# Transposing four block rows of the gated matrix between the node steps, and running 28 chunks ahead of the products

## The reference, cut to what matters

```python
h = relu(h @ W1 + b1) @ W2 + b2
x = x + relu(h)                       # end of layer 3
h = maximum(layernorm(x), 0)          # h of layer 4
xp = h @ W_node.T + b_node            # the node product
msg = gate[:, None] * xp[col]         # gate: one number per edge
out = segment_sum(msg, row) / maximum(cnt, 1)[:, None]
return x + out
```

## Time and profile before

| | us |
|---|---|
| runs (3) | 1353.11, 1356.61, 1362.15; median 1356.61 |
| the profiled execution | 1352.15, span 1350.5 |
| end of the paths to the first `turn_g` | 1133.8 to 1168.3 of the span |
| gated loop | 1168.3 to 1341.9 |
| tail: back, scale, store | 1341.9 to 1350.5 |

### The profile page before, as it was taken

How to read it: one execution, slowest core, us unless ns; L and a number is a source line. 1 busy time by engine, 2 the same in 40 slices (tenths; PEclk the granted TensorE clock), 3 DMA queues, 4 the chain that set the end, 5 groups by cost and what they waited for, 6 DMA issues and landing times. The chain is left out here.

```text
span 1350.5 us, 36825 instructions
## 1 busy us (share of the span) xinstructions
PE 1072.0 (79%) x15699; PEld 795.3 (59%) x15699; DVE 969.5 (72%) x1451; ACT 608.5 (45%) x2011; POOL 166.3 (12%) x315
## 2 busy tenths in 40 slices
PE   1495038888888887888888888839999898899997
PEld 1331026666666665666666666539999886655454
DVE  8782158999999999999999999656668724233333
ACT  1202036555555555555555555249996212122222
POOL 4130441211121112111211121000000000000000
PEclk9597557989988989898899999759999998699999
DMA  9523311231122113211321131168000070166641
GB/s 234 123 79 37 47 33 76 99 124 75 75 117 106 75 75 136 88 75 75 135 88 75 75 148 77 74 259 355 2 2 2 1 293 2 50 244 236 242 155 24
DMA packets 37038, 144.85 MB, mean 107 GB/s; under 512 B 21084, under 2 KB 21628, under 8 KB 30204
## 3 DMA queue, kind: packets, MB, share of 16 engines
q1 hardware_dynamic: 31692, 133.20, 27.2%
q0 software_dynamic: 2912, 7.92, 2.3%
q10 hardware_dynamic: 2256, 1.23, 0.4%
HBM read 78.63 MB, written 63.71 MB: 105 GB/s over the span
## 5 line engine op out<-in xcount | busy, mean ns | idle before, releaser
L869 ACT ACTIVATE b_c_row<-b_ps 128x300 bf16<-128x300 f32 (+1 forms) x275 | 114.8, 418 | 235.2 <-PE b_ps L1035 231.3
L1238 PE MATMUL layers_ps<-layers_u,layers_c 128*128 128x192 bf16 x2500 | 210.9, 247 | 8.9 <-ACT layers_u L1417 6.4
L1238 PEld LDWEIGHTS layers_ps<-layers_u,layers_c 128*128 128x128 bf16 x2500 | 208.0, 98 | 14.1 <-DVE layers_y L1546 8.0
L1035 PEld LDWEIGHTS b_ps<-b_mv,b_soh 64*128 64x128 bf16 x9600 | 171.3, 98 | 63.2 <-issue 28.6
L1035 PE MATMUL b_ps<-b_mv,b_soh 64*128 64x50 bf16 (+1 forms) x9600 | 198.4, 193 | 11.5 <-DVE b_mv L948 9.3
L1085 PE MATMUL b_ps<-k_ident,b_a_row 128*128 128x128 f32 x625 | 118.9, 314 | 89.8 <-DVE b_scale L968 88.7
L1035 PE MATMUL b_ps<-b_u_b,b_y 128*128 128x64 f32 x1250 | 165.4, 284 | 12.5 <-DVE b_y L982 12.2
L1085 PEld LDWEIGHTS b_ps<-k_ident,b_a_row 128*128 128x128 f32 x625 | 75.0, 155 | 156.5 <-DVE b_scale L968 128.1
L1035 PEld LDWEIGHTS b_ps<-b_u_b,b_y 128*128 128x128 f32 x1250 | 151.5, 196 | 18.8 <-DVE b_y L982 15.2
L948 DVE TENSOR_TENSOR b_mv<-b_mv,b_parts 128x2808 bf16<-128x2808 bf16 x100 | 149.3, 1493 | 0.0
L1693 DVE COPY layers_c<-layers_ps 128x512 f32<-128x512 f32 (+1 forms) x87 | 55.4, 636 | 117.8 <-PE layers_ps L1372 117.8
(11 more groups left out here) (237 smaller groups left out, 1142.4 us busy)
## 6 DMA issues: line engine op xcount, KB each, us to landing
g_blocks<-b_g_row SPq DMA_DIRECT2D x25, 1600.0 KB, 8.8
layers_c<-g_blocks SPq DMA_DIRECT2D x25, 1600.0 KB, 6.9
c_blocks<-b_c_row SPq DMA_DIRECT2D x25, 800.0 KB, 3.4
layers_c<-c_blocks SPq DMA_DIRECT2D x12, 1600.0 KB, 26.4
prep_attr<-in_edge_attr SPq DMA_DIRECT2D x1, 5642.0 KB
rec<-sort_rec SPq DMA_DIRECT2D x1, 1209.0 KB, 9.3
layers_c<-c_blocks SPq DMA_DIRECT2D x1, 800.0 KB, 24.9
k_xs<-in_x SPq DMA_DIRECT2D x1, 768.0 KB
```

Source lines behind the costliest of these rows:

```text
L869: nc.scalar.activation(out, src[:, :, at, :, :], ACT.Copy).then_inc(s["evac"], 1)
L1035: return nc.tensor.matmul(out, lhsT, rhs, start=start, stop=True, skip_group_check=True)
L1238: return nc.tensor.matmul(out_, lhsT, rhs, start=start, stop=True, skip_group_check=True)
```

## The change

`turn_g` and `use` of PE are defined ahead of the last steps of layer 3. Chunks 0 to 27 (block rows 0 to 3) are transposed between those steps and the node product's, into banks 0 to 3; `gt` grows from 4 to 32 places, and `across` moves behind it. The zero products that open banks 0 to 3 come after the last of these copies. PE's node steps are reordered too: the `turn` of group q + 1 stands ahead of `node(q)`. ACT and DVE copy the early chunks between their own steps, and DVE's three count instructions (L1676 to L1678) move behind them. The loop transposes q + 28 and q + 29 before it uses q and q + 1.

```diff
+AHEAD, KEEP = 28, 32
...
-        gt = [flat[:, RING * NP + 512 * i:RING * NP + 512 * i + 512] for i in range(4)]
-        across = flat[:, RING * NP + 2048:RING * NP + 4096].rearrange("p (k n) -> p k n", k=4)
+        gt = [flat[:, RING * NP + 512 * i:RING * NP + 512 * i + 512] for i in range(KEEP)]
+        across = flat[:, RING * NP + 512 * KEEP:RING * NP + 512 * KEEP + 2048].rearrange("p (k n) -> p k n", k=4)
...
@@ PE
-            turn(6, 6, "z")
-            first(5, 5)
-            first(6, 6)
-            output(5)
-            output(6)
-            for q in range(4):
-                turn(7 + q, q, "h")
-                node(q)
-            for q in range(4, 7):
-                turn(7 + q, q, "h")
-                node(q)
-            pe.wait_ge(s["took"], 4 * NP2)
-            for bank in range(4):
-                mm(ps[:, bank, :]...zeros16..., True)
...
+                bank = q % 4 + (0 if q < AHEAD else 4)
                 for j in range(nh):
-                    ins = nc.tensor.transpose(ps[:, 4 + q % 4, P * j:P * j + P], rows[b % RING][:, h0 + j, :], k["ident"][:])
+                    ins = nc.tensor.transpose(ps[:, bank, P * j:P * j + P], rows[b % RING][:, h0 + j, :], k["ident"][:])
...
+            turn(6, 6, "z")
+            pe.wait_ge(s["took"], 4 * NP2)
             turn_g(0)
             turn_g(1)
+            first(5, 5)
+            turn_g(2)
+            first(6, 6)
+            turn(7, 0, "h")
+            turn_g(3)
+            output(5)
+            turn_g(4)
+            output(6)
+            turn_g(5)
+            for q in range(7):
+                if q < 6:
+                    turn(8 + q, q + 1, "h")
+                turn_g(6 + 3 * q)
+                turn_g(7 + 3 * q)
+                node(q)
+                turn_g(8 + 3 * q)
+            turn_g(AHEAD - 1)
+            copied(AHEAD - 2)
+            copied(AHEAD - 1)
+            for bank in range(4):
+                mm(ps[:, bank, :]...zeros16..., True)
+            pe.wait_ge(s["turned"], 14)
+            pe.wait_ge(s["read"], 14)
             for q in range(0, len(steps), 2):
-                for after in (q + 2, q + 3):
+                for after in (q + AHEAD, q + AHEAD + 1):
                     if after < len(steps):
                         turn_g(after)
@@ ACT
+            def keep(q):
+                n, bank = P * CHUNKS[steps[q][1]][1], q % 4 + (0 if q < AHEAD else 4)
+                act.wait_ge(s["turn_g"], q + 1)
+                if q >= KEEP:
+                    act.wait_ge(s["used"], q - KEEP + 1)
+                nc.scalar.activation(gt[q % KEEP][:, 0:n], ps[:, bank, 0:n], ACT.Copy).then_inc(s["act_g"], 1)
+
             take(6, 1)
+            keep(0)
             hide(5)
+            keep(2)
             hide(6)
+            take(7, 4)
+            keep(4)
             square(5)
-            take(7, 4)
+            take(8, 4)
             root(5)
-            for q in range(1, 7):
-                take(7 + q, FOURS[q][1])
+            for q in range(7):
+                if 0 < q < 6:
+                    take(8 + q, FOURS[q + 1][1])
+                for g in (6 + 3 * q, 7 + 3 * q, 8 + 3 * q):
+                    if g % 2 == 0:
+                        keep(g)
+            for q in range(AHEAD, len(steps), 2):
+                keep(q)
@@ DVE (keep as on ACT, with tensor_copy and dve_g)
+            keep(1)
+            keep(3)
+            output(5)
+            output(6)
+            centre(5)
+            keep(5)
+            vary(5)
+            norm(5)
+            for q in range(7):
+                for g in (6 + 3 * q, 7 + 3 * q):
+                    if g % 2:
+                        keep(g)
+                node(q)
+                if (8 + 3 * q) % 2:
+                    keep(8 + 3 * q)
+            keep(AHEAD - 1)
             c(v.tensor_reduce(t[:], counts...))
             c(v.tensor_scalar(t[:], t[:], 1.0, None, ALU.max))
             c(v.reciprocal(dis[:], t[:]))
-            output(5)
-            output(6)
-            centre(5)
-            node(0)
-            vary(5)
-            node(1)
-            norm(5)
-            for q in range(2, 7):
-                node(q)
+            for q in range(AHEAD + 1, len(steps), 2):
+                keep(q)
```

More of the change, by code:

```diff
@@ L1343, in _ @@
             paths(pe, narrow, wide)
-            turn(6, 6, "z")
-            first(5, 5)
-            first(6, 6)
-            output(5)
-            output(6)
-            for q in range(4):
-                turn(7 + q, q, "h")
-                node(q)
-            for q in range(4, 7):
-                turn(7 + q, q, "h")
-                node(q)
-            pe.wait_ge(s["took"], 4 * NP2)
-            for bank in range(4):
-                mm(ps[:, bank, :].rearrange("p (a n) -> p a n", a=4), k["zeros16"][:], k["zeros16"][:, None, :].to_broadcast([P, 4, P]), True)
-            pe.wait_ge(s["turned"], 14)
-            pe.wait_ge(s["read"], 14)
             def copied(q):
@@ L1379, in use @@
                 n, low = P * nh, F * (i % 2)
-                mm(ps[low:low + F, i // 2, 0:n], y[:, b, :], gt[q % 4][:, 0:n], False).then_inc(s["used"], 1)
+                mm(ps[low:low + F, i // 2, 0:n], y[:, b, :], gt[q % KEEP][:, 0:n], False).then_inc(s["used"], 1)
             def back(bank):
@@ L1387, in back @@
                 ins.then_inc(s["turn_g"], 1)
+            turn(6, 6, "z")
+            pe.wait_ge(s["took"], 4 * NP2)
             turn_g(0)
             turn_g(1)
+            first(5, 5)
[18 more added lines that the diff above has]
+            for bank in range(4):
+                mm(ps[:, bank, :].rearrange("p (a n) -> p a n", a=4), k["zeros16"][:], k["zeros16"][:, None, :].to_broadcast([P, 4, P]), True)
+            pe.wait_ge(s["turned"], 14)
+            pe.wait_ge(s["read"], 14)
             for q in range(0, len(steps), 2):
-                for after in (q + 2, q + 3):
+                for after in (q + AHEAD, q + AHEAD + 1):
                     if after < len(steps):
@@ L1675, in _, with keep @@
             paths(dve, narrow, wide)
+            def keep(q):
+                n, bank = P * CHUNKS[steps[q][1]][1], q % 4 + (0 if q < AHEAD else 4)
+                dve.wait_ge(s["turn_g"], q + 1)
+                if q >= KEEP:
+                    dve.wait_ge(s["used"], q - KEEP + 1)
+                v.tensor_copy(gt[q % KEEP][:, 0:n], ps[:, bank, 0:n]).then_inc(s["dve_g"], 1)
+            keep(1)
[14 more added lines that the diff above has]
+            keep(AHEAD - 1)
             c(v.tensor_reduce(t[:], counts[:, :, :].rearrange("p b s -> p s b"), AX.X, ALU.add))
```

## The result

Four runs of the changed kernel have a median of 1337.55 us (1334.74 to 1340.08), four of the kernel before 1355.15 (1353.11 to 1362.15). The ratio is 0.986, with an interval of 0.982 to 0.990: the kernel is faster, by 1.4%. The forecast was 1340 in 1333 to 1356.6.

A forecast was written before the change was run, and what follows sets the result against it. PE alone was taken to pace the gated loop. Savings of 13.1 + 3.7 + 1.5 = 18.3 us, less 3 for half clock, gave 15.3: 1336.9 from the profiled execution, 1341.3 from the median, written 1340, range 1333 to 1356.6.

The forecast's parts named there:

- The 13.1 us of 100 transpositions: Gated loop: 100 transpositions, priced by distance of starts and not by length, leave PE's loop and save 13.1 us.
- The products cost the same in the last two periods, 1 us either way: Loop's last two periods of 14 chunks, without transpositions: products still cost 7.2 us per period, uncertain by 1 us.
- The waits in the seam: Stretch ahead of the gated loop: PE waits 0.4, 0.7, 1.4 and 0.7 us; at full clock the loop starts 3.7 earlier.
- The clock: Seam: one fall near 1148 or already after the branch's gap, a rise before the loop; two half-clock spells, 3 us.
- The sum: Whole kernel: 18.3 us at full clock less 3 for half clock, 15.3 us saved; 11 to 17 us, chance 0.40.
- The signs: First gated product at 1165 to 1170, seam clock 0.6 to 0.95, loop 159 us, longest wait node(1) for DVE's read.
- A (full clock): Rival: full clock throughout the seam, 18.3 us saved; chance 0.30.
- C (transpositions only moved): Rival: half clock throughout the seam, so the transpositions only move, 0 us saved (0 to 6); chance 0.25.
- D (half clock into the loop): Rival: half clock goes on into the loop, slower, each 4 us there costing 2.0 more; chance 0.05.
- Loads and copies cost nothing: Seam and loop: the 28 copies fit idle ACT and DVE time, loads have 15 us to spare; cost nothing.

The follow-up runs named there:

- fillers: The changed kernel with eight products of zeros queued on PE ahead of the branch: 1334.57 us, ratio 0.987 to the kernel before; again on another chip 1331.22, 0.985.
- e1_late: The changed kernel with its 28 early chunks transposed in one run behind the node steps, lead of 28 kept: 1345.88 us, ratio 0.997 to the kernel before.
- e0_after: The first profiled execution of the changed kernel, with no further edit: 1338.97 us.
- e4_batch: The runs of four: the changed kernel's loop transposes four chunks, then uses four, not two and two: 1322.53 us, ratio 0.979 to the kernel before.
- the best one: The changed kernel with zero products ahead of the branch, DVE's last norm moved later, and four chunks per run in the loop: 1321.15 us, ratio 0.976.

## Why the prediction was right

**The 13.1 us of 100 transpositions.** Right. PE's work in the seam was forecast at 26.0 us with them and measured 26.16 at full clock (fillers). In one run, partly at half clock, the 100 took 13.55 in the trace of e1_late; by length, at 0.27 each, they would have been 27. Reading the start and not the length is what carried the sum.

**The products cost the same in the last two periods, 1 us either way.** Wrong in size: 3.3 us less. The step took the 7.2 us per 14 chunks as the price of the products, while part of it is the price of being cut into pairs. The runs of four showed a turn and back as 0.30 us, of which 0.15 lies in the products. The changed loop has about 14 turns fewer, so this explains about 2 of the 3.3 us; the rest is not explained.

**The waits in the seam.** Right in place, cause and nearly in size: forecast 0.7 and 1.4, measured 0.38 and 1.25; the last 0.7, measured 0.58; that for hide(5) 0.4, measured 0.28 at full clock. Full clock was forecast to make the seam 29.2 us; with the fillers it measured 28.67 and 28.6.

**The clock.** The case was right: the prediction named a fall after node(1) or already after the branch's gap, with a rise before the loop, and priced two; both came, each with a rise again. Its size was not. I gave two spells 3 us and they cost 6.0, since each lasted 6.8 us and not the 3.7 of the loop's opening from which the price was taken. That row was read too short: the opening is only the end of a stretch at half clock, and PE had worked without a break since 1166.0, through the last node product and the zero products, 6.0 us and not 3.7. One of the changed kernel's three executions put the two spells together into one. Why the clock falls in one execution and not in another with the same gap (1.29 us at the branch, a fall in e0_after and none in e4_batch) is open.

**The sum.** Two wrong sizes of 3 us each with opposite signs: 15.3 forecast, 16.0 in the profiled execution, 17.6 between the medians. That 1340 lies within 2.5 us of 1337.55 is in part luck: 3.3 us too few for the products and 3.0 too few for the clock cancel.

**The signs.** Of those named ahead, the clock of the seam (0.80) and the longest wait (node(1) for DVE's read) came. The loop was 155.7 us and not 159. The first gated product, at 1173.91, lies outside 1165 to 1170; with the start of the seam 2.8 us later taken off it is 1171.1, about 1 us out, which is the second spell. No sign of wrong reasoning came: the loop lost 17.9 us, and its period of 14 chunks is 13.78 as before (1180.90 to 1194.68).

**The rivals.** A (full clock) is what the fillers make; it is not what the change does. C (transpositions only moved) and D (half clock into the loop) did not come: the loop entered at 1.00 in every trace. What the Trainium skill (TensorE: Matmul & The Clock Gate, "A second HAM failure mode: psum-queue depth-cycling") says of short idle times between groups and a swinging clock agrees in part: the seam of the changed kernel does swing between 0.50 and 1.00. But its first fall follows the gap at the branch and no wait for a bank, and with the fillers the waits for banks, 0.39 and 1.25 us, left the clock at 1.00.

Against C speaks most the trace of e1_late: PE did nothing but float32 transpositions from 1166.97 on, and the clock rose among them, at 1171.7.

```profile
1134.47:1168.00 33.53, 25.21 (x95) 18.48 (x96) 8.68 (x20) 5.89 (x12) 0.00 (x0) 0.50 0.01 2
1168.00:1182.00 14.00, 13.42 (x102) 12.57 (x101) 8.54 (x14) 7.62 (x14) 0.00 (x0) 0.87 0.64 250
```

What the Trainium skill (TensorE: Matmul & The Clock Gate, "Part 4: PE-mode transpose") says, that a transposition does not count as activity for the clock, does not agree with that trace (its measured case is bfloat16, of which no run here has one). The rise in the kernel before, which the prediction held against it, is weaker evidence: ahead of its 16 transpositions stood 1.7 us of zero products with no gap.

**Loads and copies cost nothing.** Right: in the traces of the changed kernel and of the best one PE waited for no load, though a block row there took only about 6.4 us (half of 13.78 - 3.5 x 0.30), less than the 7.0 to 7.1 of a load. Loads of several rows are under way ahead of use in the ring of six, and only the changed kernel and shorter loops down to 6.4 us a row were tried.

## What to carry to other kernels

Where one engine paces a loop, look for work that can be done ahead of the loop in a stretch where that engine waits; the trace prices it by the distance of starts, and here the lead itself was worth little. Then look at how often the engine changes between kinds of work: longer runs of each, as far as the banks reach, gave here 9.9 us more, over half of what the whole change gave. A stretch that mixes waits with work is to be priced at both clock levels, and a short idle time of 1 to 2 us just ahead of it can be worth filling: here that gave 6.0 us in the profiled seam, 0 and 3 us between medians.

## What the runs showed of the hardware that was not expected

Changing between full-width float32 transpositions and half-width products costs PE 0.30 us for each turn and back, though PE is shown busy throughout: 154.74 us of loop against 142.73 with 37 fewer turns (and 0.9 us of transpositions more ahead of its first product), in nine traces of the one and two of the other, each the same to the hundredth.

Products queued on PE just ahead of a branch ran while the branch was under way: PE's idle time of 1.29 to 1.78 us became 0.42 to 0.78, the way through the branch grew by about 0.8 us for 1.9 us of products, and the clock stayed at 1.00 through the seam in all five traces with them. Without them it fell at the seam's start in four of the five traces that have the early transpositions (in that of the runs of four it fell later, at 1144.5, for 10.2 us).

The clock rose from 0.50 to 1.00 in the middle of a run of 100 float32 transpositions, 4.7 us after their start (e1_late).
